# Four column tiles for the attending products, and a depthwise layer in split fp32r products with its sums in PSUM

## What is computed

```python
# layer 0, the part that matters: 2 groups of 2 heads, 256 sampled keys
attn = softmax(einsum('bcm,bcn->bmn', q, k) * scale + bias)   # 4096 queries x 256 keys per head
out  = einsum('bmn,bcn->bcm', attn, v)                        # 32 channels per head
return conv1x1(out, wo)

# layer 2
x_33  = dwconv3x3(x)
x_15  = dwconv5x1(dwconv1x5(x))
x_111 = dwconv11x1(dwconv1x11(x))
return (conv1x1(x_33 + x_15 + x_111, w3) + b3) * x
```

## Time and profile before

| | us |
|---|---|
| median of 3 runs | 6795.28 (6787.41 to 6802.78) |
| the profiled execution's own time | 6799.16 |
| its span, first to last instruction | 6797.1 |
| PE busy | 5450.1 (80%) |
| DVE busy | 4483.5 (66%) |
| POOL busy | 2301.0 |
| ACT busy | 2062.3 |
| mean granted TensorE clock | 0.907 |

### The profile page before, as it was taken

One profiled execution on the slowest core, in us unless ns is written; L12 is line 12 of the kernel. 1 busy time (PEld: TensorE's weight loads), 2 busy tenths in 40 slices (PEclk: granted clock), 3 DMA queues, 4 the chain that ended last, 5 costly groups with the idle time before them and its releaser, 6 DMA issues. The chain is left out here.

```text
span 6797.1 us, 125088 instructions
## 1 busy us (share of the span) xinstructions
PE 5450.1 (80%) x48621; PEld 4102.8 (60%) x48621; DVE 4483.5 (66%) x7316; ACT 2062.3 (30%) x3979; POOL 2301.0 (34%) x1228
## 2 busy tenths in 40 slices
PE   3878787878787785195775969999969999999991
PEld 2646555555555463174564824444459999999991
DVE  5766766766667675687787589999933333455553
ACT  2656565666556563132222212111100000000000
POOL 1544354544535353274665534554400000000000
PEclk9989898989888897597988979999979999999995
DMA  3000000000000001232221101001030000000005
GB/s 127 15 27 27 27 17 24 22 19 27 14 27 14 27 15 48 63 97 68 80 86 54 47 29 50 25 25 50 12 137 0 0 0 0 0 0 0 0 0 185
DMA packets 78550, 251.90 MB, mean 37 GB/s; under 512 B 25248, under 2 KB 26528, under 8 KB 67872
## 3 DMA queue, kind: packets, MB, share of 16 engines
q1 hardware_dynamic: 78112, 246.07, 10.5%
HBM read 139.49 MB, written 67.11 MB: 30 GB/s over the span
## 5 line engine op out<-in xcount | busy, mean ns | idle before, releaser
L2198 DVE SCALAR_TENSOR_TENSOR l_state<-l_conv,l_state 128x256 f32 x500 | 292.7, 585 | 783.3 <-PE l_conv L2134 783.3
L517 POOL TENSOR_TENSOR l_probs<-l_probs,l_inv 128x1024 f32<-128x1024 f32 x256 | 495.6, 1940 | 625.3 <-DVE l_inv L926 624.7
L1900 PE MATMUL l_mix<-l_mid,l_fold 128*128 128x512 f32 x1408 | 632.2, 606 | 79.0 <-DVE l_mid L1996 78.7
L1428 PE MATMUL l_gather_ps<-l_wdiag,l_stage 128*128 128x128 f32 x4608 | 547.1, 279 | 163.9 <-DVE l_wdiag L1583 163.8
L1428 PEld LDWEIGHTS l_gather_ps<-l_wdiag,l_stage 128*128 128x128 f32 x4608 | 537.1, 195 | 208.0 <-issue 150.1
L1996 DVE SCALAR_TENSOR_TENSOR l_mid<-l_xpad,l_w,l_mid 128x1024 f32<-128x1024 f32 x448 | 635.7, 1441 | 2.3
L2134 PE MATMUL l_conv<-l_carry_hi,l_taps_lo 128*128 128x248 f32 (+2 forms) x4500 | 624.8, 284 | 0.0
L2134 PE MATMUL l_conv<-l_carry_hi,l_taps_hi 128*128 128x248 f32 (+2 forms) x4500 | 621.8, 282 | 2.9 <-DVE l_carry_hi L2164 2.0
L2134 PE MATMUL l_conv<-l_carry_lo,l_taps_hi 128*128 128x248 f32 (+2 forms) x4500 | 619.6, 282 | 0.0
L2134 PEld LDWEIGHTS l_conv<-l_carry_hi,l_taps_lo 128*128 128x128 f32 x4500 | 577.9, 190 | 0.0
L2134 PEld LDWEIGHTS l_conv<-l_carry_hi,l_taps_hi 128*128 128x128 f32 x4500 | 575.6, 189 | 3.3 <-DVE l_carry_hi L2164 2.2
(11 more groups left out here) (267 smaller groups left out, 8880.2 us busy)
## 6 DMA issues: line engine op xcount, KB each, us to landing
l_xleft<-l_xt SPq DMA_DIRECT2D x64, 283.5 KB
l_xright<-l_xt SPq DMA_DIRECT2D x64, 283.5 KB
stat_xs<-in_x SPq DMA_DIRECT2D x8, 2048.0 KB, 23.2
l_hats<-in_x SPq DMA_DIRECT2D x8, 2048.0 KB, 7.6
l_xraw<-in_x SPq DMA_DIRECT2D x8, 2048.0 KB, 9.0
after_layer<-l_xraw SPq DMA_DIRECT2D x64, 256.0 KB, 2.0
l_xblk<-after_layer SPq DMA_DIRECT2D x32, 512.0 KB, 4.6
l_xres<-after_layer SPq DMA_DIRECT2D x32, 512.0 KB, 4.3
```

The costliest lines, as they stand in the source:

```text
L517: pool.tensor_tensor(part, part, inv[:, u, cols].rearrange("c (j o) -> c j o", o=1).to_broadcast([C, 4, KEYS]), ALU.mult).then_inc(scaled_ ...
L1428: last = pe.matmul(gather_ps[u][y // 4][:, y % 4 * C:(y % 4 + 1) * C], stage[:, u, y + k // 3, :], wdiag[:, y % SLOTS, k, :], start=(k == ...
L1900: pe.matmul(bank[:, :], fold11[:, j, :], flat(mid11[:, r + j:r + j + ROWS, :]), start=(j == 0), stop=False)
L2198: dve.scalar_tensor_tensor(row, conv[h][:, 0:HB * W].rearrange("c (b w) -> c b w", b=HB), 0.0, row, op0=ALU.max, op1=ALU.add).then_inc(lin ...
```

## The change

In layer 0 each of the four products of `attend` gets 32 PSUM rows of its own, so that they lie in four column tiles and nothing accumulates. `copy_out` copies all 128 rows to a new buffer `attended`, and the sum over the two key halves is taken in `mix`, whose weights `wo4` hold each group's rows twice. So `mix` and `accumulate` now run for group 0 too. Preparing `wo4` takes two small copies and one more transpose.

```diff
-                            last = pe.matmul(bank[out_bank][at, :], vals[:, t, at],
-                                             probsT[:, o % 2, t, h, :, :].rearrange("c k n -> c (k n)"), start=(t == 0), stop=(t == 1))
+                            rows = slice(DH * (2 * t + h), DH * (2 * t + h + 1))
+                            last = pe.matmul(bank[out_bank][rows, :], vals[:, t, at], probsT[:, o % 2, t, h, :, :].rearrange("c k n -> c (k n)"),
+                                             start=True, stop=True)
...
-                    pe.matmul(bank[mix_bank], woT[:, :], q[:, queries(o)], start=True, stop=True).then_inc(mixed, 1)
+                    pe.matmul(bank[mix_bank], wo4[:, g, :], attended[:, o % 2, :], start=True, stop=True).then_inc(mixed, 1)
...
-                        if g and n >= 5 and n % 2:
-                            mix((n - 5) // 2)
-                mix(OCTS - 1)
+                        if n >= 5 and n % 2:
+                            mix(g, (n - 5) // 2)
+                    mix(g, OCTS - 1)
...
-                        if g and n >= 6 and n % 2 == 0:
-                            accumulate((n - 6) // 2)
+                        if n >= 6 and n % 2 == 0:
+                            accumulate(g, (n - 6) // 2)
```

```diff
+            def add33(i, s, blk, *products):
+                for j in products:
+                    pool.wait_ge(made33, count(i, s, BLOCKS * ADDS, blk * ADDS + j + 1))
...
+                    pool.tensor_tensor(part33(blk), part33(blk), rows(prod33[:, j % PRODUCTS, :]), ALU.add).then_inc(added33, 1)
...
+            def batch(i, s):                      # POOL
+                for blk in range(BLOCKS):
+                    due = list(behind(i, s, blk, LAG))
+                    add33(i, s, blk, 0, 1, 2)
+                    for j, t, k in due[:1]:
+                        gate(j, t, k)
+                    add33(i, s, blk, 3, 4)
+                    for j, t, k in due[1:]:
+                        gate(j, t, k)
+                    add33(i, s, blk, 5, 6, 7)
...
+                pe.matmul(bank[:, :], w3T[:, :], flat(sum33[:, r:r + ROWS, :]), start=True, stop=False)
+                for p, (weights, five, eleven) in enumerate(((fold_hi, hi5, hi11), (fold_lo, hi5, hi11), (fold_hi, lo5, lo11))):
+                    for j in range(11):
+                        last = pe.matmul(bank[:, :], weights[:, 5 + j, :], flat(eleven[:, r + j:r + j + ROWS, :]), start=False, stop=False)
...
+            def products33(i, s, blk, *products):  # ACT
+                for j in products:
+                    tap, src = taps_of_33(s, blk)[j + 1]
+                    before = blk * ADDS + j + 1 - PRODUCTS
+                    if j < PRODUCTS:
+                        before = blk * ADDS
+                    wait(act, added33, count(i, s, BLOCKS * ADDS, before))
+                    act.activation(rows(prod33[:, j % PRODUCTS, :]), src, ACT.Identity, scale=tap).then_inc(made33, 1)
...
+            def batch(i, s, last=False):           # ACT
+                for blk in range(BLOCKS):
...
+                    firsts(i, s, blk)
+                    products33(i, s, blk, 0, 1, 2)
+                    for j, t, k in behind(i, s, blk, LAG):
+                        evacuate(j, t, k)
+                    if blk == BLOCKS - 1 and not last:
+                        norm(i + s, 1 - s)
+                    products33(i, s, blk, 3, 4)
+                    high11(i, s, blk)
+                    products33(i, s, blk, 5)
+                    high5(i, s, blk)
+                    products33(i, s, blk, 6, 7)
...
+            def batch(i, s):                       # DVE
+                for blk in range(BLOCKS):
+                    sum_taps(i, s, blk, rows(acc11[:, :]), taps_of_11(s, blk), 12 * blk, first11, taps11_done)
+                    sum_taps(i, s, blk, rows(acc5[:, :]), taps_of_5(s, blk), 12 * blk + 9, first5, taps5_done)
+                    dve.wait_ge(hi11_done, count(i, s, BLOCKS, blk + 1))
+                    dve.tensor_tensor(part11(lo11, blk), rows(acc11[:, :]), part11(hi11, blk), ALU.subtract).then_inc(lo11_done, 1)
+                    for j, t, k in behind(i, s, blk, LAG + 2):
+                        stats(j, t, k)
+                    dve.wait_ge(hi5_done, count(i, s, BLOCKS, blk + 1))
+                    dve.tensor_tensor(part5(lo5, blk), rows(acc5[:, :]), part5(hi5, blk), ALU.subtract).then_inc(lo5_done, 1)
```

More of the change, by code:

```diff
@@ L358, in _ @@
                 dve.tensor_copy(wvT[:, :], bank[2][:, 0:C])
-                dve.tensor_copy(woT[:, :], bank[3][:, 0:C])
+                for g in range(GROUPS):
+                    dve.tensor_copy(wo4[:, g, :], bank[3 + g][:, 0:C])
         waits_met = mem.sem("waits_met")
@@ L1853, in _ @@
                 store(ROUNDS - 1, s)
[L1854 to L1855 removed]
+            for k in range(CHUNKS):
+                sp.wait_ge(stored[k], 16 * B)
         @block.gpsimd
@@ L1877, in _ @@
+            for s in range(2):
+                batch(0, s)
+            with pool.Fori(1, ROUNDS) as i:
+                for s in range(2):
+                    batch(i, s)
+            for k in range(CHUNKS - LAG, CHUNKS):
+                gate(ROUNDS - 1, 1, k)
         @block.tensor
@@ L1917, in norm @@
                                scale=sh.rstd[:, bass.ds(n, 1)], bias=sh.shift[:, bass.ds(n, 1)]).then_inc(normed[s], 1)
-            def first(i, s, blk):
-                n = i * 2 + s
-                wait(act, mixed, (n - 1) * CHUNKS + chunks_read(blk))
-                for acc, bias, terms in tap_sums(s, blk * BROWS):
-                    tap, src = terms[0]
-                    more = {} if bias is None else {"bias": bias}
-                    act.activation(acc, src, ACT.Identity, scale=tap, **more).then_inc(first_taps, 1)
@@ L1947, in _ @@
             act.wait_ge(weights_loaded, LOADS)
+            act.wait_ge(pads_zero, 1)
             norm(0, 0)
-            act.wait_ge(normed[0], 1)
-            for blk in range(BLOCKS):
-                first(0, 0, blk)
-            norm(0, 1)
+            act.wait_ge(fold_made, 1)
+            act.activation(fold_hi[:, :, :], fold, ACT.Copy).then_inc(fold_hi_made, 1)
             act.wait_ge(mix_bias_ready, 1)
-            evacuate(0, 0)
-            with act.Fori(1, ROUNDS) as i:
-                norm(i, 0)
-                evacuate(i - 1, 1)
-                norm(i, 1)
-                evacuate(i, 0)
@@ L1960, in _ @@
-            evacuate(ROUNDS - 1, 1, ahead=False)
+            act.wait_ge(folds_ready, 1)
+            batch(0, 0)
+            batch(0, 1)
+            with act.Fori(1, ROUNDS - 1) as i:
+                batch(i, 0)
+                batch(i, 1)
+            batch(ROUNDS - 1, 0)
+            batch(ROUNDS - 1, 1, last=True)
+            for k in range(CHUNKS - LAG, CHUNKS):
+                evacuate(ROUNDS - 1, 1, k)
         @block.vector
         def _(dve):
+            zero = sh.ident[:, 0:1].to_broadcast([C, P11 * W])
@@ L2016, in _ @@
-            batch(0, 1)
-            stats(0, 0)
-            chain.end()
-            with dve.Fori(1, ROUNDS) as i:
-                chain.start(i)
-                batch(i, 0)
-                stats(i * 2 - 1, 1)
-                batch(i, 1)
-                stats(i * 2, 0)
-                chain.end()
-            stats(B - 1, 1)
+            dve.tensor_tensor(mix_bias[:, :], mix[0][:, C:C + 1], biases[:, 5:6], ALU.add).then_inc(mix_bias_ready, 1)
+            dve.wait_ge(fold_made, 1)
+            dve.wait_ge(fold_hi_made, 1)
@@ new lines, in _, with sum_taps @@
+            dve.tensor_tensor(fold_lo[:, :, :], fold, fold_hi[:, :, :], ALU.subtract).then_inc(folds_ready, 1)
+            def sum_taps(i, s, blk, acc, taps, before, first, done):
+                dve.wait_ge(first, count(i, s, BLOCKS, blk + 1))
+                for j in range(1, len(taps)):
+                    tap, src = taps[j]
+                    if j > 1:
+                        dve.wait_ge(tap_chain, count(i, s, BLOCKS * 12, before + j - 1))
+                    last = dve.scalar_tensor_tensor(acc, src, tap, acc, op0=ALU.mult, op1=ALU.add)
+                    if j < len(taps) - 1:
+                        last.then_inc(tap_chain, 1)
+                last.then_inc(done, 1)
@@ L2028, in layer3 @@
+            for s in range(2):
+                batch(0, s)
+            with dve.Fori(1, ROUNDS) as i:
+                for s in range(2):
+                    batch(i, s)
+            for k in range(CHUNKS - LAG - 2, CHUNKS):
+                stats(ROUNDS - 1, 1, k)
 def layer3(nc, sh, x_in, w_dirs, out):
```

273 lines of the change are left out of this document (152 added, 121 removed).

## The result

The changed kernel takes 6557.61 us in the median (6553.68 to 6559.4), against 6791.34 for the one before: a ratio of 0.9654 (0.9637 to 0.967). The forecast was 6580 in a range of 6500 to 6690; both of its terms were off in size, one each way. The profiled execution took 6553.68 us, of which the span is 6552.0, 245.1 less than the span before.

What follows compares the result with a forecast made beforehand. DVE bounded layer 2, PE just behind; afterwards POOL would, at 25.5 us a round. Layer 2 -185 and layer 0 -30 make -215: 6799 - 215 - 4 = 6580 us, range 6500 to 6690.

Steps and rivals of the forecast that it cites:

- GpSimd sets the round of layer 2: Layer 2: POOL is the longest and sets the pace of each 16-row block, 25.5 us against 22.8 and 22.6.
- The size of that round: Layer 2, per 16-row block on POOL: additions 19.2, gates 5.2, bubble 1.15, together 25.5 us (22.0 to 27.0).
- the stand: Layer 2: POOL stands still once a round, for one product and the handover, 1.15 us.
- the ends of the layer: Layer 2: first additions some 4.4 us later; at the end PE's chunks 22.9, evacuation 0.69, gate 2.58, statistics 0.69.
- over 90%: Layer 2: sign that POOL sets the pace, its busy share of the layer.
- DVE with ACT 22.8, PE 22.6: Layer 2: us a round beside POOL's; rival that DVE and ACT set it: total 6502, chance 0.10.
- Additions in PSUM: Layer 2, DVE: taken to cost as in SBUF; rival at 1.8 us a step: total about 6715, chance 0.12.
- POOL and DVE exclude one another: Layer 2, slower rival: their times in a round add to 46.4 us, layer 2 +440, total 7200, chance 0.05.
- Layer 0, the octet of group 1: Layer 0: attend over four tiles takes 0.98 us in place of 1.84, a gain of 0.86 an octet.
- Layer 0, group 0: Layer 0: new mix set against saved attend and PE's slack; 0 taken, between -4 and +5 us an image.
- The clock: Layer 0: PE's clock rises later from half, 1.7 us in 16 openings, +27 us, between 0 and 90.
- 58 - 27 - 1: Layer 0: gain 58, later clock 27, wo4 copies 1; net -30 us, between -90 and +60.

Runs made afterwards that it cites:

- the kernel with two passes: Changed kernel with the low part of the folded weights and its 16 matmuls per chunk left out of layer 2: 6534.49 us.
- the early product: Changed kernel, but in layer 2 ScalarE makes a block's first product as soon as its slot is free, one addition earlier: 6515.36 us (ratio 0.959).
- the thin product of group 0: Changed kernel with the mixing product of layer 0's first group cut to 16 of its 512 columns: 6540.43 us.

## Why the prediction was right

Its mechanism held in layer 2 and in group 1 of layer 0. That the total came within 22 us is partly luck: layer 2 gave 25 us less than said and layer 0 some 50 more. Layer 0's 83 us against a forecast of 30 are near the end of its bounds (90), and the term for group 0 was wrong.

- **GpSimd sets the round of layer 2**: shown, by its own stand taken away (42 of 43.5 us back) and by PE's work cut by nearly a third (a round shorter by 0.16).
- **The size of that round**: 25.5 forecast, 26.3 measured. By terms, from the rows of the round: eight additions took 8.88 - 1.36 + 7.52 + 4.85 = 19.9 (19.2 forecast: I had 2.33 and 0.07 from one to the next, it is 2.41 and up to 0.1), two gates 5.05 (5.2), the stand 1.36 (1.15). 0.8 us in 32 rounds is the 25 us, and the ends of the layer add nothing to it: the first addition began 26.3 us after the layer's first instruction, where the forecast had 26.2, and the last gate ended 27.9 after the last addition (27). The mis-sized term is the addition: 2.33 lies under the least of its nearest row (2.339; the median is 2.359), which the median would have mended by 0.2 us a round of the missing 0.7. The rest is that these additions take 2.41 and follow one another less closely. Over the whole layer POOL is busy for 778 of 887 us, 88% where the forecast had over 90%.
- **DVE with ACT 22.8, PE 22.6**: DVE's chain is 18.29 us until the first subtraction (18.3 forecast). PE's round is 24.1 to 24.3, since an fp32r matmul of 512 columns follows the next after 0.234 us and not 0.218: the term stood at the low end of its bounds, 0.216 to 0.244, and was wrong by 0.016, near what carrying over the 0.015 us of the earlier trace rows would have given (0.228). It cost nothing here, as PE had 2 us of cover, but it decides the next step: with POOL relieved, PE sets a round of 24.1 us where the forecast saw 22.8 for DVE and ACT.
- **Additions in PSUM**: 1.290 us against 1.273. The Trainium skill's price for them ("VectorE: DVE Perf Modes", TRN2 errata) was 120 fixed cycles against 58. By it an addition would take 0.065 us more, an estimate; the trace shows 0.017, and 0.008 where the sum is read from PSUM and written to SBUF, so the measurement decides against it.
- **POOL and DVE exclude one another**, the slower rival with 0.05: it did not occur, and the mechanism is real. The sums' place alone decides. With them in SBUF the kernel with two passes is 492 us slower, slower than the kernel before. The forecast read it off two rows, the 14.2 us gates and the undisturbed L517, which was enough.
- **Layer 0, the octet of group 1**: 0.86 forecast, 0.98 measured. The four tiles gave 0.84; the shorter wait was not foreseen.
- **Layer 0, group 0**: 0 forecast, and this term failed. Its attention took 65.7 to 67.2 us in seven images of the trace before, 66.4 in the mean, and takes 62.9 now: 3.5 us an image, 28 in all. The forecast let POOL's scaling and hats fill the octet; the waits of the earlier trace rows took in some three fifths of the mixing product. Another 0.8 us an image in the mean are gained between the groups, for which I have no cause.
- **The clock**: its direction was right in group 1, where half clock lasts 20.5 us in place of 13.7, and wrong in group 0, where it stays at 13.7. The allowance was 1.7 us on all 16 openings, 27 in all; measured are 2.1 to 2.8 us on the eight of group 1, 17 to 22 in all. Group 1's attention took 73.2 us in the mean before and takes 66.9 now, 6.3 less. Without the late rise it would be 8.4 to 9.1 less, where the forecast had 7.3.

By these parts layer 0 gave 8 x (3.5 + 6.3 + 0.8) = 85 us less some setup, where the forecast had 58 - 27 - 1.

## What to carry to other kernels

Before work is moved to GpSimd, look at what VectorE reads beside it: with one SBUF operand the two ran freely, with two they very nearly took turns, and having the running sums in PSUM was worth 492 us, measured on the kernel with two passes. After a change that brings three engines near one another (POOL, PE and DVE had 26.3, 24.3 and 21.8 us of each round), one wait on the longest of them comes back whole (1.36 us x 32), and the next engine stops the gain soon after (24.1 us a round): price all three to the last tenth, from medians. Column tiles pay when the products that they separate are independent; adding two halves in the product that follows anyway, with its weights stacked twice, costs nothing on that product (1.12 us with 128 rows as with 64).

## What the hardware showed unexpectedly

- VectorE and GpSimd in each other's way don't lose alike: VectorE's addition doubles (1.29 to 2.62 us in the mean), GpSimd's grows by a third (2.39 to 3.26).
- A write of VectorE to SBUF with one operand from PSUM leaves GpSimd alone (2.391 us), and is slightly quicker than the one to PSUM (1.281 for 1.290).
- With four column tiles group 1 opens at half clock for 20.5 us instead of 13.7, in which PE was busy for 20.23; group 0 with the same attends stayed at 13.7 (13.33 busy). The same group 1 has the short stretch in one image of eight with the early product and in four of eight with the thin product of group 0. What tells them apart is open.
